# A three-layer CIN kernel on one core: chunk 0's b from TensorE, one multiply per group, and two of layer 3's groups split in all four tiles

## The reference

```python
for (W, b), split in zip(conv_params, split_flags):      # three layers, split True, True, False
    z = jnp.einsum('bhd,bmd->bhmd', x, x0).reshape(B, h * x0.shape[1], D)
    xk = jax.nn.relu(jnp.einsum('oc,bcd->bod', W, z) + b[None, :, None])
    if split:
        half = xk.shape[1] // 2
        x, xk = (xk[:, :half], xk[:, half:])
    else:
        x = xk
    results.append(xk)
y = jnp.sum(jnp.concatenate(results, axis=1), axis=2) @ Wo.T + bo
```

## Time and profile before

| | |
|---|---|
| time, median of three runs | 475.0 us (474.65 to 475.0) |
| the profiled execution | 474.85 us, span 472.9 us |
| TensorE matmuls | 443.7 us busy, 94% |
| TensorE weight loads | 299.8 us, 63% |
| VectorE | 430.4 us, 91% |
| GpSimd | 407.2 us, 86% |
| ScalarE | 318.4 us, 67% |
| transfers | 76.84 MB, 162 GB/s on average |

### The profile page before, as it was taken

How to read it: one execution, slowest core, us unless ns; L and a number is a source line. 1 busy time by engine, 2 the same in 40 slices (tenths; PEclk the granted TensorE clock), 3 DMA queues, 4 the chain that set the end, 5 groups by cost and what they waited for, 6 DMA issues and landing times.

```text
span 472.9 us, 5975 instructions
## 1 busy us (share of the span) xinstructions
PE 443.7 (94%) x1600; PEld 299.8 (63%) x1600; DVE 430.4 (91%) x490; ACT 318.4 (67%) x397; POOL 407.2 (86%) x147
## 2 busy tenths in 40 slices
PE   0796999899999999999999999999999999999997
PEld 0243556466767767676767766676766767677774
DVE  1499996988999999999999999999999999999997
ACT  1456785576868777585868767685877768577761
POOL 0145698589999999999999999999999999999995
PEclk9998999999999999999999999999999999999999
DMA  8999829999995959779495969969495962922010
GB/s 215 251 253 213 178 53 223 223 206 217 200 225 114 233 116 225 155 170 229 102 228 114 222 133 206 194 138 228 115 229 119 227 143 66 201 44 46 21 23 1
DMA packets 22608, 76.84 MB, mean 162 GB/s; under 512 B 5827, under 2 KB 5827, under 8 KB 18116
## 3 DMA queue, kind: packets, MB, share of 16 engines
q1 hardware_dynamic: 22596, 76.70, 74.0%
HBM read 61.48 MB, written 0.00 MB: 130 GB/s over the span
## 4 chain that ended last, share of the span: by engine, by line
PE 76%; DMA 9%; DVE 4%; SPq 4%; POOL 3%; issue 2%; ACT 2%; DVEq 0%; POOLq 0%
PE y_ps L784 24%; PE y_ps L790 14%; PE y_ps L772 14%; PE y_ps L774 14%; PE y_ps L780 6%; DMA shifted<-xt_dram 6%; PE y_ps L796 3%; POOL zl L553 3%; DVE z L602 2%; DMA a_rep<-x_sb 2%; DMA b_fac<-xt_dram 1%; SPq L335 1%; SPq L319 1%; SPq L344 1%; SPq L321 1%
## 5 line engine op out<-in xcount | busy, mean ns | idle before, releaser
L553 POOL TENSOR_TENSOR zl<-z,zh 128x1024 fp32r<-128x1024 f32 (+1 forms) x141 | 405.2, 2908 | 48.9 <-ACT zh L470 48.7
L602 DVE TENSOR_TENSOR z<-a_ps,b_fac 128x512 f32<-128x512 f32 (+2 forms) x256 | 272.3, 1086 | 25.5 <-PE y_ps L796 11.9
L470 ACT ACTIVATE zh<-z 128x1024 fp32r<-128x1024 f32 (+1 forms) x141 | 176.3, 1251 | 118.4 <-DVE z L602 117.9
L790 PE MATMUL y_ps<-zl,w_high 128*128 128x512 f32 x330 | 152.2, 554 | 6.2 <-POOL zl L553 6.2
L772 PE MATMUL y_ps<-zh,w_high 128*128 128x512 f32 x330 | 130.8, 396 | 4.7 <-ACT zh L470 3.8
L774 PE MATMUL y_ps<-zh,w_low 128*128 128x512 f32 x330 | 129.1, 391 | 0.0
L784 PE MATMUL y_ps<-z,w_raw 128*128 128x512 f32 x252 | 128.4, 591 | 0.0
L790 PEld LDWEIGHTS y_ps<-zl,w_high 128*128 128x128 f32 x330 | 61.5, 188 | 75.6 <-issue 58.7
L772 PEld LDWEIGHTS y_ps<-zh,w_high 128*128 128x128 f32 x330 | 61.9, 188 | 21.4 <-issue 3.6
L774 PEld LDWEIGHTS y_ps<-zh,w_low 128*128 128x128 f32 x330 | 62.1, 188 | 13.4
L784 PEld LDWEIGHTS y_ps<-z,w_raw 128*128 128x128 f32 x252 | 47.3, 188 | 10.4
(11 more groups left out here) (42 smaller groups left out, 176.9 us busy)
## 6 DMA issues: line engine op xcount, KB each, us to landing
b_fac<-xt_dram SPq DMA_DIRECT2D x52, 512.0 KB, 8.7
shifted<-xt_dram SPq DMA_DIRECT2D x64, 256.0 KB, 4.9
a_rep<-x_sb SPq DMA_DIRECT2D x87, 128.0 KB, 2.4
shifted<-xt_dram SPq DMA_DIRECT2D x64, 128.0 KB, 5.1
b_fac<-xt_dram SPq DMA_DIRECT2D x24, 256.0 KB, 9.4
a_rep<-x_sb SPq DMA_DIRECT2D x58, 64.0 KB, 2.1
w_raw<-w_dram SPq DMA_DIRECT2D x2, 640.0 KB, 13.6
w_raw<-w_dram SPq DMA_DIRECT2D x2, 384.0 KB, 17.3
```

Source lines behind the costliest of these rows:

```text
L470: nc.scalar.activation(zh[:, slot, 0:end - native, :], z[:, slot, native:end, :], ACT.Copy).then_inc(zh_ready, 1)
L553: nc.gpsimd.tensor_tensor(zl[:, slot, 0:end - native, :], z[:, slot, native:end, :], zh[:, slot, 0:end - native, :].bitcast(F32), ALU.subtract
L602: return nc.vector.tensor_tensor(dst, factor.unsqueeze(1).to_broadcast(list(dst.shape)), others, ALU.mult)
L790: mm = nc.tensor.matmul(y, wh[layer][:, w, :], zl[:, slot, t, :], start=False, stop=end_here)
```

## The change

Constants: layer 3's groups 6 and 8 split all four tiles, one of them by VectorE; all products into PSUM alternate between two banks.

```diff
-SPLIT = {1: (2,), 2: (3, 3, 3, 3), 3: (3, 3, 3, 3)}
-BY_DVE = {1: (1,), 2: (1, 0, 1, 0), 3: (1, 0, 1, 0)}
-ZX_BANK = {0: 1, 1: 0, 3: 1, 5: 0, 7: 1}
+SPLIT = {1: (2,), 2: (3, 3, 3, 3), 3: (3, 4, 3, 4)}
+BY_DVE = {1: (1,), 2: (1, 0, 1, 0), 3: (1, 1, 1, 1)}
+ZX_BANK = {0: 0, 1: 1, 3: 0, 5: 0, 6: 1, 7: 0, 8: 1}
+FOURTH = {6: 0, 8: 1}
```

```diff
-                pool = POOL_TILE[layer] if by_dve else native
-                multiply(z[:, slot, native:end, :], factor, others[:, pool:pool + end - native, :]).then_inc(z_ready, 1)
+                if layer > 1:
+                    multiply(z[:, slot, 0:end, :], factor, others[:, 0:end, :]).then_inc(z_ready, 1)
+                else:
+                    pool = POOL_TILE[layer][g]
+                    multiply(z[:, slot, native:end, :], factor, others[:, pool:pool + end - native, :]
+                             ).then_inc(z_ready, 1)
                 if by_dve:
...
-                multiply(z[:, slot, 0:native, :], factor, others[:, 0:native, :]).then_inc(z_native_ready, 1)
+                if layer == 1:
+                    multiply(z[:, slot, 0:native, :], factor, others[:, 0:native, :]).then_inc(z_front_ready, 1)
...
+                waiting = left_over(i - 1) if not isinstance(i, int) or i > 0 else None
                 for pos in positions(i):
                     if pos in here:
-                        product(i, *here[pos])
-                    if before in here and before in ZX_BANK and not is_native(here[before][0][3]):
-                        subtract(i, *here[before])
-                    before = pos
+                        product(i, *here[pos], 1 if waiting else 0)
+                    if waiting:
+                        subtract(*waiting)
+                    waiting = (i, *here[pos]) if pos in here and here[pos][0][0] in ZX_BANK and not is_native(
+                        here[pos][0][3]) else None
```

```diff
+            def pick_b(half):
+                for j in range(GT * half, GT * half + GT):
+                    if half:
+                        pe.wait_ge(b0_made, j - GT + 1)
+                    nc.tensor.matmul(pick_banks[j % GT], pick_sb[:, j, :], shifted[0:Q, XREP * CH:(XREP + 1) * CH],
+                                     start=True, stop=True).then_inc(b0_picked, 1)
+            pe.wait_ge(zeros_set, 1)
+            for _ in range(2):
+                nc.tensor.matmul(y_ps[2][:], pooled3[:, 0:P], pooled3[:], start=True, stop=True)
+            pe.wait_ge(fields_loaded, 16)
+            pe.wait_ge(pick_loaded, 16)
+            pick_b(0)
             def body(i):
+                if i_is(i, 1):
+                    pick_b(1)
```

ScalarE's four copies of the second half stand in pass 0 between the two halves of a. The transfers:

```diff
+            load_ends(0, 0, 0, fields_loaded)
+            sp.dma_start(pick_sb, pick).then_inc(pick_loaded, 16)
             load_x(0)
...
             load_w(2, w2, 0)
-            load_b_half(0, 0)
-            load_b_half(0, 1)
             load_w(2, w2, 1)
             load_x(1)
+            sp.wait_ge(b0_picked, 2 * GT)
             load_w(3, w3, 0)
...
             load_x(3)
+            load_b_half(2, 0)
+            load_b_half(2, 1)
...
-                if i_is(i, 2):
-                    load_b_half(2, 0)
-                    load_b_half(2, 1)
```

More of the change, by code:

```diff
@@ L266, in cin_kernel @@
         x_loaded = sem("x_loaded")
-        b_half_loaded = [(sem(f"b{c}_loaded"), sem(f"b{c}_rest_loaded")) for c in range(HALVED)]
+        fields_loaded = sem("fields_loaded")
+        pick_loaded = sem("pick_loaded")
+        b0_picked = sem("b0_picked")
+        b0_made = sem("b0_made")
+        b_half_loaded = {c: (sem(f"b{c}_loaded"), sem(f"b{c}_rest_loaded")) for c in range(1, HALVED)}
         b_loaded = sem("b_loaded")
@@ L473, in body @@
                             act.wait_ge(zx_ready, e + 1)
-                            nc.scalar.activation(zh[:, slot, end - native, :], zx_ps[:, ZX_BANK[pos], :], ACT.Copy
+                            nc.scalar.activation(dve_part("high", pos, slot, end - native), zx_ps[:, ZX_BANK[pos], :], ACT.Copy
                                                  ).then_inc(zxh_ready, 1)
@@ L603, in multiply, with product @@
                                                ALU.mult)
-            def product(i, step, k):
+            def product(i, step, k, held):
                 pos, layer, g, q, e = step
@@ L765, in body @@
                     by_pool = end - native - QUARTER[layer]
-                    pool = POOL_TILE[layer] if by_dve else native
+                    pool = POOL_TILE[layer][g] if by_dve else native
                     places = [(t, splits.index((g, pool + t))) for t in range(by_pool)]
@@ L779, in body @@
                         for weights in (wh, wl):
-                            nc.tensor.matmul(y, weights[layer][:, x_weights, :], zh[:, slot, x_part, :],
+                            nc.tensor.matmul(y, weights[layer][:, x_weights, :], dve_part("high", pos, slot, x_part),
                                              start=False, stop=False)
-                    pe.wait_ge(z_native_ready, q + 1)
+                    if layer == 1:
+                        pe.wait_ge(z_front_ready, c + NATIVE_GROUPS)
                     for t in range(native):
@@ L795, in body @@
                         pe.wait_ge(zxl_ready, e + 1)
-                        mm = nc.tensor.matmul(y, wh[layer][:, x_weights, :], zl[:, slot, x_part, :],
+                        mm = nc.tensor.matmul(y, wh[layer][:, x_weights, :], dve_part("low", pos, slot, x_part),
                                               start=False, stop=last)
@@ L806, in _ @@
             pe.wait_ge(terms_made, 3)
-            nc.tensor.matmul(y_ps[1][0:1, 0:EARLY], ones[:], terms[:], start=True, stop=True).then_inc(out_summed, 1)
+            nc.tensor.matmul(y_ps[1][0:1, 0:EARLY], ones[:], terms, start=True, stop=True).then_inc(out_summed, 1)
             pe.wait_ge(last_begun, 1)
```

92 lines of the change are left out of this document (60 added, 32 removed).

## The result

| | kernel before | kernel after |
|---|---|---|
| median of the runs (lowest to highest) | 474.82 us (474.33 to 475.0, 4 runs) | 480.87 us (480.12 to 481.01, 4 runs) |
| profiled execution: time, span | 474.85, 472.9 | 480.12, 478.3 |
| one pass (product 0 to product 0, pass 8 to 15, by seven) | 26.92 | 27.44 |
| product 0 of pass 4 | 104.01 | 101.48 |
| product 0 of pass 15 to the end of the span | 71.48 | 74.92 |

The ratio is 1.0126, 95% interval 1.0108 to 1.0143: slower by some 1.3%. The three last rows of the table carry it: -2.5 up to pass 4, +4.5 in the eleven passes from there, +3.4 at the end.

What follows compares the result with a forecast made beforehand. TensorE was taken to pace the old kernel, a cross-engine loop the new. Product 0 of pass 4 at 101.8 plus 11 passes of 27.45, then the end, made +3.5 on the profiled 474.85: median 478.4, range 470.5 to 482.

Steps and rivals of the forecast that it cites:

- The loop: Steady passes: a loop through VectorE, GpSimd's groups 2 to 6 and TensorE grows by 1.30, making each pass 27.45 us.
- What would show it: Signs in the steady passes: pass 27.3 to 27.5, TensorE idling some 0.8 a pass, GpSimd idling 1.6 ahead of group 2.
- Rival B: Steady passes: TensorE keeps the pace at 26.58 a pass, time 467 us; chance 0.15.
- The start: Passes 0 to 3: terms sum to -2.2, product 0 of pass 4 at 101.8 instead of 104.01, bounds 99 and 105.
- The later first product: Start of chunk 0: two more transfers ahead of x delay the first product by 0.6, between 0 and 1.1.
- The copies: Start, ScalarE: four copies of the second picks, 0.6 each, partly beside VectorE's work, cost +0.7, bounds 0 and 2.4.
- The load waits: Pass 3: earlier issue of chunk 2's loads shortens VectorE's waits for b and ScalarE's for a: -3, between 0 and -5.
- The clock term: Layer 1 of chunk 0: early TensorE matmuls may raise its clock before the first records: -1.5, bounds 0 and -2.9.
- The end: From product 0 of pass 15 on: GpSimd's later row +1.0 and one more matmul +0.23.
- GpSimd's later row: Last passes: GpSimd's row of groups begins 1.0 later than before and carries the last two passes, +1.0.
- the last group: End of the kernel: the very last group has one matmul more, +0.23.

Runs made afterwards that it cites:

- pair of undone splits: Two runs on the kernel after, giving layer 3's group 6, or group 8, its native fp32 tile back: 477.61 and 472.67 us.
- pooling later: Kernel after with VectorE's reduction for layers 1 and 2 moved from ahead of product 2 to behind it, nothing added or removed: 473.91 us, ratio 0.9985.
- start alone: Kernel after with groups 6 and 8 native again and every native tile but group 8's multiplied on its own, new start kept: 470.51 us, ratio 0.9912.
- group 8 native again: Kernel after with group 8 given one native tile and three for GpSimd again, group 6 still split in four: 472.67 us, ratio 0.9960.

## Why the prediction was right, and where it was off

The predicted 478.4 stands against 480.87, at the upper edge of the forecast's own 475 to 481; on the profiled execution 478.3 against 480.12. By its own steps:

- **The loop** was right in each piece. Product 0 to product 2 6.92 (6.46 + 0.60 - 0.06, less 0.05, is 6.95); product 2 to GpSimd's group 2 3.88 (3.35 + 0.53); its groups 2 to 6 15.21 (15.22); from there to product 0 1.47 (1.17 + 0.23 = 1.40). Pass 27.44, predicted 27.45. The pair of undone splits shows that it is the loop and not VectorE's sum of work; the order-only run shows it once more.
- **What would show it.** GpSimd idles ahead of group 2 once a pass, 1.74 where I had 1.6. TensorE's gaps of 0.8 a pass can't be seen in its busy time (0.8 in 236 us), since a record's modelled end of 0.40 covers more than its step of 0.23. The weight loads show them. From 164 to 400 us they wait 46 times for GpSimd, in the kernel before never; a weight load runs ahead of its matmul (below, the load at 236.63 belongs to the matmul at 236.87), so the sum of these waits is more than TensorE loses:

```profile
PEld y_ps L857 <- POOL zl L588: 21.8, 46, 0.9
```

  Here one ahead of the zl matmuls of group 6:

```profile
236.63 0.19 PEld L846 LDWEIGHTS y_ps<-zh_fourth,w_low 128*128 128x128 f32 x1
237.37 0.53 PEld L857 LDWEIGHTS y_ps<-zl,w_high 128*128 128x128 f32 x3 [0.55 <-POOL zl L588]
```

- **Rival B**, TensorE at 26.58, fell twice. With the loop in its way the pass was 27.44, and with the loop out of the way the pass with both splits is 26.81, not 26.58. I had named a rule for it: the Trainium skill's "Perfetto Trace Analysis", section "Identifying the Most-Contended Engine", optimizes the engine with the highest occupancy first, but judges TensorE's headroom by its arithmetic and the busy share of its weight loads, not by that of its matmuls. I had left the second half out: by weight loads TensorE is at 70% (164.71 of 236), and VectorE and GpSimd, at 96%, would have come first. The measurements speak for TensorE all the same: the chain that ended last is 76% TensorE before, and one native matmul fewer a pass gave 0.13 once the loop was out of the way. What no ranking of engines shows is the loop. Relieving TensorE lost 0.52 a pass here, because the relief was paid ahead of GpSimd's longest row. It is the run "pooling later", which relieves nobody, that gave 0.58 back.
- **The start**: product 0 of pass 4 at 101.48, predicted 101.8. That it came so near is luck: single terms were off and cancelled. The later first product cost 1.0 (11.29), not 0.6; in the eleven traces with this order of loads it lies between 10.58 and 11.71. The copies cost next to nothing (product 1 to product 3 5.43, before 5.36), not 0.7. By product 0 of passes 1 and 2 all of this was gone: 37.72 and 57.55, before 37.62 and 57.46. But product 5 of pass 2 had been late (44.36, before 40.49) and with it GpSimd's row of groups; VectorE then waits 0.66 and 0.56 for TensorE, where it had no such wait, ScalarE copies x at 74.60 instead of 72.17, and product 0 of pass 3 comes at 75.21 instead of 72.79: +2.4, where I had +1. The run "start alone" has the same 17.7 between these two products, so it is not the splits; which of the moves in the start does it was not tried. The load waits gave more than -3: pass 3 took 26.27 instead of 31.22, -5.0, the end of my bound. What let them go was right in kind (transfers issued earlier), wrong in its cause: I put it down to chunk 0's b no longer holding the queue. x of chunk 1 did let SyncE go on 8 us earlier, as I had said (23.59, before 32.08), and with chunk 0's b loaded again, SyncE going on at 31.35, nothing was lost. It was the place of b of chunk 2 ahead of SyncE's wait, and I had read that wait without looking at what the queue did just before it.
- **The clock term** of -1.5 had no ground. The records' time came out as predicted (5.23 against 6.66), and product 1 at 21.05 instead of 21.51 in spite of a first product 1.0 later, which looked like a hit. It is chance of the execution: ten traces that begin with the same matmuls of zeros and picks have these records at 5.15 to 6.49, and one without any matmul ahead of them has 5.32. Nor did it reach the time: product 0 of pass 1 is where it was.
- **The end** is the term that was mis-sized: 1.2 predicted, 3.4 measured. I had +1.0 for GpSimd's later row, +0.23 for the last group, and "the extra subtraction there lies beside GpSimd". The first two are there: from product 0 of pass 15 to group 2 10.80 instead of 9.80, and from GpSimd's end to the end of the span 5.39 instead of 5.12. The third is wrong. In passes 16 and 17 there is no product 0 behind which group 8's subtraction could wait for ScalarE, and VectorE stands still in front of product 1 and, in pass 17, of product 5. VectorE of the kernel after:

```profile
431.79 0.69 DVE L706 TENSOR_TENSOR zl_fourth<-zx_ps,zh_fourth 128x512 fp32r<-128x512 f32 x1 [1.26 <-ACT zh_fourth L506]
...
456.31 0.69 DVE L706 TENSOR_TENSOR zl_fourth<-zx_ps,zh_fourth 128x512 fp32r<-128x512 f32 x1 [0.85 <-ACT zh_fourth L506]
...
469.86 0.69 DVE L706 TENSOR_TENSOR zl_fourth<-zx_ps,zh_fourth 128x512 fp32r<-128x512 f32 x1 [0.84 <-ACT zh_fourth L506]
```

GpSimd's stops of 2.43 against 0.27 are the missing 2.2, and with it the whole difference between 478.3 and 480.1 (+2.2, less 0.3 at the start, less 0.1 around the span). The subtraction accounts for some 1.3 of them: with group 8 native again the stops are 1.16, and the end 2.4 shorter (1.27 of stops, 0.54 ahead of group 2, 0.60 behind GpSimd's end). The other 0.9 doesn't need it: with the start alone, no group split in four, the stops are 1.18 too. Which of the edits that it shares with the kernel after makes them is open.

## What to carry to other kernels

Where several engines are over 95% busy and a ring of a few buffers ties them, take work off the fullest one only after you have laid out the ring's loop and seen where the work lands: the same subtraction cost 0.2 us a pass behind the long row of GpSimd and 0.5 in front of it, and moving a reduction of 0.68 without removing it was worth 0.58. A merged instruction saves its fixed part (0.06 here) and gives its first consumer everything late (0.53 here). Before engineering bytes away from a full queue, look for a stretch in which it is empty, and for what stands in front of the issuing engine there: moving two lines was worth 6.1 us, and no version of the change did better (469.09 at best, against 468.48).

## What the runs showed of the hardware

- TensorE's first clock rise differs from execution to execution. Over fourteen traces (the twelve experiments' and the two kernels'), layer 1's eight records of chunk 0 took 5.15 to 6.66 us (0.43 each at 2.4 GHz would be 3.4, 0.83 at 1.2 GHz 6.66), and VectorE's product 1 started at 20.11 to 22.50. Kernels with a busy TensorE from 1.35 us on lie at both ends (5.15 and 6.49). And an early rise was paid back: in all seven traces with the first records at 5.68 or less, layer 2's sixteen took 8.80 to 8.83, as the clock fell once more under them (granted 0.81 from 24 to 30 us in the kernel after, 0.88 in the one without any warming); in the other seven, 6.06 or more, they took 7.10 to 7.13 (granted 1.00 in the kernel before). A term that rests on one trace's clock in the first 30 us is worth nothing.
- A matmul whose weights have 32 rows takes what one with 128 takes. The picks at the full clock, of the kernel after:

```profile
20.74 1.02 PE L782 MATMUL x_ps<-shifted,w_raw 32*128 32x512 f32 x2
21.60 1.02 PE L782 MATMUL y_ps<-shifted,w_raw 32*128 32x512 f32 x2
```

  One follows the other by 0.86, as an fp32 matmul of 128 rows does in the earlier trace rows. This is what the Trainium skill's "TensorE: Matmul & The Clock Gate", section "Why this matters for your kernels", says, and this case's trace agrees.
- In these traces a VectorE instruction with both operands in SBUF and GpSimd's subtraction (its operands lie there too) took turns, and the one that started first ran at its own pace. The subtraction of 128x768 of the weights starts 0.06 ahead of GpSimd's in the kernel before and takes 0.95, while GpSimd's 1024 columns take 3.14 instead of 2.40:

```profile
29.21 0.95 DVE L564 TENSOR_TENSOR w_low<-w_raw,w_high 128x768 fp32r<-128x768 f32 x1
29.27 3.14 POOL L553 TENSOR_TENSOR zl<-z,zh 128x1024 fp32r<-128x1024 f32 x1 [15.68 <-ACT zh L470]
```

  Behind GpSimd's, in the same trace, it takes 3.59:

```profile
33.42 3.46 POOL L553 TENSOR_TENSOR zl<-z,zh 128x1536 fp32r<-128x1536 f32 x1 [1.02 <-ACT zh L470]
34.11 3.59 DVE L564 TENSOR_TENSOR w_low<-w_raw,w_high 128x768 fp32r<-128x768 f32 x1 [1.09 <-ACT w_high L453]
```

  It ends 0.8 behind the end of GpSimd's, as if it had only begun there, and so do the other three of 128x768 that start behind one of GpSimd's in the two traces. The two of 128x896, which the change moved, took 2.06 (GpSimd's was still running for 1.1) and 1.08 (GpSimd idle).
